# Sequence-mixing block and window attention on one core: start of the scan by half sequences, B of four units in float32, split of B, decay ring and mlp additions in another order

## What is computed

```
block 0 (per image, L = 1024 positions, E = 192 inner channels, N = 16 states)
  xn  = layernorm over channels(x) * gamma + beta          # forward and reversed: 8 sequences
  xr  = silu(causal conv of 4 taps(xn @ W_in[:, :E]) + conv_b);   z = xn @ W_in[:, E:]
  dbl = xr @ W_xproj                                       # rank 6 | B (16) | C (16)
  dt  = softplus(dbl[:6] @ W_dt + b_dt)
  h_t = exp(dt_t * A[n]) * h_(t-1) + dt_t * xr_t * B_t[n]    # for each channel and state n
  y_t = sum over n of C_t[n] * h_t[n] + D * xr_t
  x   = x + 0.5 * (forward + reversed)((y * silu(z)) @ W_out)
block 1 (4 images, 6 heads of 16 channels)
  qkv = conv1x1(batchnorm(x)); scores = 7x7 conv of (q, k) -> 49 weights per head and position
  out = softmax(scores) . the 7x7 window of v; x = x + proj(out); x = x + c2(gelu(c1(x)))
```

## Time and profile before

| | before |
|---|---|
| median of 3 runs | 1159.88 us |
| the profiled execution, its own time | 1160.85 us |
| its span | 1159.1 us |
| first scan of unit 0 starts | 59.52 us |
| last scan (unit 191) starts | 745.79 us |
| attention's first instruction | 756.17 us |
| mean granted TensorE clock | 0.944 |
| PE, DVE, ACT, POOL busy | 1048.3, 919.1, 571.7, 918.2 us |

### The profile page before, as it was taken

How to read it: one execution, slowest core, us unless ns; L and a number is a source line. 1 busy time by engine, 2 the same in 40 slices (tenths; PEclk the granted TensorE clock), 3 DMA queues, 4 the chain that set the end, 5 groups by cost and what they waited for, 6 DMA issues and landing times. The chain is left out here.

```text
span 1159.1 us, 9592 instructions
## 1 busy us (share of the span) xinstructions
PE 1048.3 (90%) x3268; PEld 371.8 (32%) x3268; DVE 919.1 (79%) x598; ACT 571.7 (49%) x601; POOL 918.2 (79%) x369
## 2 busy tenths in 40 slices
PE   7889999899999999998987888979999999997865
PEld 2223333233333323333333323323333333332321
DVE  1299998869998989998898999920197978979881
ACT  5766859598866666766667654322112020110411
POOL 0079999989998979999899998610098999899890
PEclk8879999989999989999999999969999999999778
DMA  3234556633555554755354655368475678936002
GB/s 86 95 125 148 191 158 168 196 135 128 201 171 160 163 168 130 187 165 201 127 198 140 190 160 195 113 145 174 86 138 126 120 143 152 159 69 107 23 0 77
DMA packets 112769, 162.78 MB, mean 140 GB/s; under 512 B 63962, under 2 KB 76992, under 8 KB 112720
## 3 DMA queue, kind: packets, MB, share of 16 engines
q1 hardware_dynamic: 109264, 155.17, 50.2%
q10 hardware_dynamic: 3456, 6.99, 2.1%
HBM read 137.43 MB, written 11.23 MB: 128 GB/s over the span
## 5 line engine op out<-in xcount | busy, mean ns | idle before, releaser
L750 POOL TENSOR_TENSOR hc<-h,c_rep 128x1024 f32<-128x1024 f32 x191 | 447.2, 2359 | 104.4 <-DVE h L803 93.1
L803 DVE TENSOR_TENSOR_SCAN h<-a,bu 128x1024 f32<-128x1024 f32 x192 | 436.8, 2284 | 31.9 <-ACT bu L631 9.8
L452 PE MATMUL y_ps<-hc,ident 128*128 128x512 f32 x768 | 380.7, 620 | 0.8 <-DVE hc L851 0.3
L621 ACT ACTIVATE a<-dt,a_neg 128x1024 f32<-128x1024 f32 x192 | 216.6, 1143 | 133.7 <-DVE h L803 130.9
L790 DVE TENSOR_TENSOR bu<-bu,u 128x1024 f32<-128x1024 f32 x165 | 199.6, 1210 | 20.9 <-PE bu L422 20.8
L452 PEld LDWEIGHTS y_ps<-hc,ident 128*128 128x128 f32 x768 | 144.8, 195 | 203.0 <-issue 183.2
L1248 POOL TENSOR_TENSOR prod_p<-vw,at 128x3584 f32<-128x3584 f32 x18 | 130.4, 7243 | 93.5 <-ACT at L1209 92.2
L1128 PE MATMUL sc_ps<-x,w_up 128*64 128x480 f32 (+3 forms) x672 | 142.9, 576 | 0.0
L1128 PE MATMUL sc_ps<-x,w_low 96*64 96x480 f32 (+6 forms) x672 | 136.5, 556 | 0.0
L422 PE MATMUL bu<-st,pick 96*128 96x512 bf16 (+1 forms) x438 | 101.5, 389 | 35.9 <-DVE h L803 34.2
L1198 ACT ACTIVATE sc<-sc_ps,rel 128x512 f32<-128x512 f32 x24 | 16.5, 687 | 237.8 <-PE sc_ps L1128 237.8
(11 more groups left out here) (129 smaller groups left out, 993.4 us busy)
## 6 DMA issues: line engine op xcount, KB each, us to landing
c_rep<-bc_d SPq DMA_DIRECT2D x128, 512.0 KB, 3.8
c_rep<-bc_d SPq DMA_DIRECT2D x128, 256.0 KB, 4.0
vw<-v_d SPq DMA_DIRECT2D x24, 532.0 KB, 9.3
x<-qk SPq DMA_DIRECT2D x66, 140.0 KB, 3.9
b_rep<-bc_d SPq DMA_DIRECT2D x17, 512.0 KB, 4.8
b_rep<-bc_d SPq DMA_DIRECT2D x20, 256.0 KB, 5.1
scores_d<-sc ACTq DMA_DIRECT2D x48, 98.0 KB
at<-scores_d SPq DMA_DIRECT2D x48, 98.0 KB, 3.9
```

The costliest lines, as they stand in the source:

```text
L452: mm = pe.matmul(y_ps[:, cols(th)], ident[:, :], hc[:, k % HC_RING, cols(th)], start=(n == 0 and d == 0), stop=(n == N_ST - 1))
L621: nc.scalar.activation(a[:, k % A_RING, :], dt[:, tile % 2, :], ACT.Exp, scale=a_neg[:, kind_of(tile), n:n + 1]).then_inc(exp_done, 1)
L750: nc.gpsimd.tensor_tensor(hc[:, k % HC_RING, :], h[:, k % H_RING, :], c_rep[:, k % C_RING, :], ALU.mult).then_inc(hc_done, 1)
L803: nc.vector.tensor_tensor_scan(scan_order(h[:, k % H_RING, :], d), scan_order(a[:, k % A_RING, :], d), scan_order(bu[:, k % 2, :], d), 0.0 ...
```

## The change

1. The loads: the first group keeps x of image 0 and `center`; gamma and beta go to the second.
2. The start by half sequences (512 positions): squares and scalings on DVE, Ln, Exp and the affine on ACT by halves; a second buffer `var_1` (it lies in `hc`) for image 1; `w_taps` is made by POOL instead of DVE; conv of tile 0's first half is issued before the variance of image 1; tile 2's silu is taken straight out of PSUM by halves; softplus of tile 0 by halves on ACT and DVE, with its u.
3. Units 0 to 3 spread B from `dbc` in float32 with `pick_f` (two matmuls), so they need no split; the split of sequence 0 is made by ACT and POOL behind the first two decays, in buffers of its own (`st_left` lies in `hc`). conv of tile 1 still stands before the first spread in PE's queue.
4. `A_RING` 3 to 4: the decay is issued three units ahead instead of two.
5. `PLAN`: xp and dt of sequence 1 / tile 1 one unit later. `middle` 5 units after its job instead of 2, `lowest` 6 instead of 2 (for the job's end at unit e: `rest` e+1, `middle` e+5, `lowest` e+6); `affine` 4 instead of 3; B of the POOL units loaded and multiplied four units ahead instead of three.
6. Attention: `mlp_out` sits behind a row's product; image 0's first pair goes from after tile 4 to row (4, 3), its second pair from after the tile to row (5, 0), image 1's first pair from row (5, 0) to (5, 1); image 2's last pair from before to after the division of tile 5. The sum of the weights and its reciprocal come after row 0.

```diff
-A_RING, H_RING, HC_RING, C_RING, SUM_LAG = 3, 4, 4, 4, 3
+A_RING, H_RING, HC_RING, C_RING, SUM_LAG = 4, 4, 4, 4, 3
-LOADS = [4, 7, 12, 8]
+LOADS = [2, 9, 12, 8]
-DVE_MLP = {(4, WIN): ((0, 0),), (4, WIN + 1): ((0, 8),), (5, 0): ((1, 0),), (5, 2): ((1, 8),), (5, 3): ((2, 0),),
-           (5, WIN): ((2, 8),)}
+DVE_MLP = {(4, 3): ((0, 0),), (5, 0): ((0, 8),), (5, 1): ((1, 0),), (5, 2): ((1, 8),), (5, 3): ((2, 0),)}
-    (0, "xp", 1, 0, 0), (2, "xp", 1, 0, 1), (5, "dt", 1, 0), (6, "dt", 1, 1), (7, "conv", 3, 0), (11, "conv", 3, 1),
+    (1, "xp", 1, 0, 0), (3, "xp", 1, 0, 1), (6, "dt", 1, 0), (7, "dt", 1, 1), (7, "conv", 3, 0), (11, "conv", 3, 1),
-B_RING, B_AHEAD, B_LOAD = 2, 3, 3
+B_RING, B_AHEAD, B_LOAD = 2, 4, 4
+MID_LAG, LOWEST_LAG = 5, 6
...
+                if k < EARLY:
+                    for th in range(2):
+                        mm = pe.matmul(bu[:, k % 2, cols(th)], pick_f[0:2 * N_ST, n:n + 1].to_broadcast([2 * N_ST, 128]),
+                                       dbc[0:2 * N_ST, 0, cols(th)], start=True, stop=True)
+                    mm.then_inc(spread, 1)
+                    return
...
+            for th in range(2):
+                norm_job("cen", 0, th)
+            for th in range(2):
+                norm_job("var", 0, th)
+            pe.wait_ge(loaded[1], 16 * LOADS[1])
+            for th in range(2):
+                norm_job("cen", 1, th)
+            pe.wait_ge(taps_ready, 2)
+            for j in range(TAPS):
+                conv_job(0, 0, j)
+            for th in range(2):
+                norm_job("var", 1, th)
+            for tile, th in ((0, 1), (2, 0), (2, 1)):
+                for j in range(TAPS):
+                    conv_job(tile, th, j)
...
+            def soft_half_logs(th):
+                half = cols(th)
+                act.wait_ge(job_done, J("dt", 0, th))
+                nc.scalar.activation(t3[:, half], bank("dt", 0, th), ACT.Abs, bias=b_dt[:, 0:1]).then_inc(abs_half, 1)
+                act.wait_ge(abs_half, th + 1)
+                nc.scalar.activation(t3[:, half], t3[:, half], ACT.Exp, scale=-1.0).then_inc(soft_act, 1)
+                nc.scalar.activation(dt[:, 0, half], bank("dt", 0, th), ACT.Relu, bias=b_dt[:, 0:1])\
+                    .then_inc(left_act, 1)
+                act.wait_ge(soft_act, 2 * th + 1)
+                nc.scalar.activation(t4[:, half], t3[:, half], ACT.Ln, bias=1.0).then_inc(soft_act, 1)
...
             for th in range(2):
                 center_left(0, th)
             for th in range(2):
-                variance_left(0, th)
+                variance_half(0, th)
+            act.wait_ge(loaded[1], 16 * LOADS[1])
             for th in range(2):
                 center_left(1, th)
-            affine(0)
-            for th in range(2):
-                variance_left(1, th)
-            affine(1)
+                affine_half(0, th)
...
+            conv_left(0, 0)
+            for th in range(2):
+                variance_half(1, th)
+            for th in range(2):
+                affine_half(1, th)
+            conv_left(0, 1)
+            silu(0)
+            for th in range(2):
+                leave(("conv", 2, th), xr_of(2)[:, cols(th)], bank("conv", 2, th), ACT.Silu, bias=conv_b[:, 1:2])
+            nc.scalar.preload_act_table_set("natural_log_exp_and_others")
+            for th in range(2):
+                xp_left(0, 0, th)
+            for th in range(2):
+                soft_half_logs(th)
+            nc.scalar.activation(st[:, 0, :], dbc[0:ROWS - RANK, 0, :], ACT.Copy).then_inc(st_high, 1)
             act.wait_ge(set_up, 3)
+            for k in range(2):
+                decay(k)
             middle(0, 0)
             for th in range(2):
                 conv_left(1, th)
+            for k in range(2, A_RING - 1):
+                decay(k)
             silu(1)
             nc.scalar.preload_act_table_set("natural_log_exp_and_others")
             for k in range(UNITS):
                 copy_y(k)
                 copy_b(k + 1)
-                decay(k + 2)
+                decay(k + A_RING - 1)
                 front(k)
...
-                    if done + 2 == k and name == "xp" and job[2] == 1:
+                    if done + MID_LAG == k and name == "xp" and job[2] == 1:
                         middle(*job[0:2])
...
-                        if done + 2 == k:
+                        if done + LOWEST_LAG == k:
                             lowest(nc.gpsimd, pool, SEQS.index(tuple(job[0:2])))
...
+            pool.wait_ge(loaded[1], 16 * LOADS[1])
+            for part in range(2):
+                j = slice(2 * part, 2 * part + 2)
+                nc.gpsimd.tensor_tensor(w_taps[:, j, :], conv_w_rows[:, j, :],
+                                        w_in.unsqueeze(1).broadcast_to([C, 2, E_IN]), ALU.mult)\
+                    .then_inc(taps_ready, 1)
+            rest(nc.gpsimd, pool, 0)
+            lowest(nc.gpsimd, pool, 0)
+            pool.wait_ge(st_done, 1)
...
                 for dy in range(DVE_ROWS[j]):
-                    for m, i in DVE_MLP.get((j, dy), ()):
-                        mlp_out(m, i)
-                        mlp_out(m, i + 1)
                     row(j, dy)
-                for m, i in DVE_MLP.get((j, WIN), ()):
-                    mlp_out(m, i)
-                    mlp_out(m, i + 1)
+                    if dy == 0:
+                        nc.vector.tensor_reduce(den[:, 0, :], at[:, j % 2].rearrange("p k x -> p x k"), AX.X, ALU.add)\
+                            .then_inc(soft, 1)
+                        dve.wait_ge(soft, 3 * j + 2)
+                        nc.vector.reciprocal(den[:, 1, :], den[:, 0, :]).then_inc(soft, 1)
...
-            for i in (0, 1, 8, 9):
-                mlp_out(B - 1, i)
+            for m, i in ((2, 8), (2, 9), (3, 0), (3, 1), (3, 8), (3, 9)):
+                mlp_out(m, i)
```

More of the change, by code:

```diff
@@ L229, in left, with x_ready @@
             eng.wait_ge(left_dve if JOBS[n - 1][0] == "out" else left_act, len(same))
+        def x_ready(eng, t):
+            if t == 2:
+                left(eng, J("conv", 2, 1))
+            else:
+                eng.wait_ge(xr_ready, max(CONVS.index(t), 1))
         def xr_of(t):
@@ L243, in _ @@
             groups = [
-                [(x1[:, 0, :], t["x"][0]), (center[:, :, :], t["center"]), (norm[:, 0:1], t["gamma"]),
-                 (norm[:, 1:2], t["beta"])],
-                [(x1[:, 1, :], t["x"][1]),
+                [(x1[:, 0, :], t["x"][0]), (center[:, :, :], t["center"])],
+                [(x1[:, 1, :], t["x"][1]), (norm[:, 0:1], t["gamma"]), (norm[:, 1:2], t["beta"]),
                  (conv_w_rows.rearrange("p j e -> p (j e)"), t["conv_w"].to_broadcast([C, TAPS * E_IN])),
@@ L317, in norm_job @@
                     pe.wait_ge(squared, 2 * b + th + 1)
-                    pe.matmul(bank(name, b, th)[0:C, :], center[:, 1, :], var[:, cols(th)], start=True,
+                    squares = var_1 if b == 1 else var
+                    pe.matmul(bank(name, b, th)[0:C, :], center[:, 1, :], squares[:, cols(th)], start=True,
                               stop=True).then_inc(job_done, 1)
@@ L327, in conv_job @@
                     free(J("conv", tile, th))
-                    pe.wait_ge(normalised, (i if kind == "L" else 2 * i + 1) + 1)
+                    b = i if kind == "L" else 2 * i + 1
+                    if b >= 2:
+                        pe.wait_ge(normalised, b - 1)
+                    elif tile < 3:
+                        pe.wait_ge(normal_half, 2 * b + th + 1)
+                    else:
+                        pe.wait_ge(normal_half, 2 * b + 2)
                 if kind == "L":
@@ L413, in spread_b @@
                 tile, n = divmod(k, N_ST)
-                if n == 0:
+                if n == 0 and tile or k == EARLY:
                     for s in tile_seqs(tile):
@@ L515, in variance_left, with variance_half, affine_half @@
                     nc.scalar.activation(var[:, :], var[:, :], ACT.Exp, scale=-0.5).then_inc(inverse, 1)
+            def variance_half(b, th):
+                half = (var_1 if b == 1 else var)[:, cols(th)]
+                leave(("var", b, th), half, bank("var", b, th)[0:C, :], ACT.Ln, bias=norm[:, 2:3])
+                left(act, J("var", b, th))
+                nc.scalar.activation(half, half, ACT.Exp, scale=-0.5).then_inc(inverse_half, 1)
+            def affine_half(b, th):
+                act.wait_ge(scaled_half, 2 * b + th + 1)
+                nc.scalar.activation(xi(b, cols(th)), xi(b, cols(th)), ACT.Identity, scale=norm[:, 0:1],
+                                     bias=norm[:, 1:2]).then_inc(normal_half, 1)
+            def soft_half_logs(th):
[8 more added lines that the diff above has]
+                nc.scalar.activation(t4[:, half], t3[:, half], ACT.Ln, bias=1.0).then_inc(soft_act, 1)
             def affine(b):
-                act.wait_ge(scaled, b + 1)
+                act.wait_ge(scaled, b - 1)
```

(23 more changed lines are left out.)

116 lines of the change are left out of this document (69 added, 47 removed).

## The result

The changed kernel takes **1142.73 us**, the median of 4 runs (1141.05 to 1144.43); the kernel before, run beside it on the same chip, 1159.96. The ratio is 0.985, with an interval of 0.983 to 0.9869. On the profiled executions it went from 1160.85 to 1141.05 us, and the span from 1159.1 to 1139.2.

The account below looks back on a forecast made before the run. Bound by a start chain alternating engines, nearly full DVE and POOL with stalls in the scan stage, then PE and POOL in attention. 10.5 - 0.5 + 11 - 2.2 + 2.1 + 0.7 = 21.6 less: 1138.3 us median, range 1128 to 1150.

Parts of the forecast that it names:

- (a): Start: PE's first matmul waits for `center` instead of beta, so 4.3 us instead of 5.29.
- (b): Start: norm by halves, four half tiles of conv at 3.55 us each; ends at 30.2 against 35.33.
- (e): Start: conv of tile 1 from 36.7, 10.25 or 7.1 us long; first scan 9.5 to 12.7 earlier, 10.5 taken.
- Rival (2): All fits: full clock in conv of tile 1 and the projection, scan stage gains 17; 1128.9 us, chance 0.15.
- (d): Start: softplus of tile 0 by halves; u complete at 42.6 us instead of 54.12.
- (f): Units 0 to 3: float32 spreads take 1.75 us at full clock, 3.5 at half; cost 0 to 3, 0.5 taken.
- Rival (4): Start gives its gain back: half-clock spreads and PE's backlog hold units 1 to 8; about 1153.3 us, chance 0.10.
- (h): Tile 1: softplus one unit later with `lowest` among it; a stall of 3.3 us, net 2.2 slower.
- (g): Scan stage: ACT no longer waits for POOL's `rest`, DVE's stalls shrink; 0 to 23 us gained, 11 taken.
- rival 1: Scan stage: POOL takes over and gives DVE's stalls back; gain 2 instead of 11, 1147.3 us, chance 0.22.
- (i) and (j): Attention, tile 5: POOL ends 3.1 us earlier, DVE waits 4.7 for image 1's last pair; 2.1 gained.
- (k): End of attention: image 3's projection comes packed behind image 2's mlp; 0 to 1.4 us more, 0.7 taken.

Follow-up runs that it names:

- lags: Kernel before with only the middle part of the split five units after its xp job and the lowest six, instead of two; 1147.52 us, ratio 0.9914.
- old plan: Changed kernel with xp and dt of sequence 1 / tile 1 at the units of before (0, 2, 5, 6); 1138.98 us, ratio 0.9836.
- `EARLY` = 2: Changed kernel with float32 spreads of B for units 0 and 1 only, instead of 0 to 3; 1138.24 us, ratio 0.9819.
- Put together: Changed kernel, unit 0's spread ahead of tile 1's conv, POOL's subtraction behind u, two float32 spreads, tile 1's xp and dt units of before; 1132.4 us.

## Why the prediction was right, and where it was off

The direction, the size and the condition on the distance from the first scan to the last (668 to 686; it is 676.64) held. Its other condition did not: it called itself wrong if the first scan came later than 52, and that came at 54.11. Step by step:

**(a) to (e), the start: 10.5 taken, 5.4 measured.** (a) held, 4.55 against 4.3. The term that was mis-sized is the first half tile of conv in (b): 3.55 taken from PE at full clock, 5.71 measured, since the clock had not yet risen. Where it rose at 13.9 the same half tile takes 3.67, and the first scan of the same start is at 52.09 (old plan): 2 us of the miss are this, and still less than the forecast is gained. The other way round, the 59.52 of before is of an execution in which the clock fell again; against the 56.1 of the kernels with lags or attention alone, whose start is the same, the 5.4 is 2.0. conv of tile 1 began at 40.58 instead of 36.7, and (e)'s slow end of 10.25 held (10.18). Rival (2) had this conv at full clock and 12.7 instead of 10.5. It was not: the wait ahead of it was 1.16 us for the 1.3 foreseen, the granted clock was 1.00 in 28 to 36 us and 0.50 in 40 to 44, and this conv took 10.10 to 10.59 us in all eight other executions with the new start. That fewer waits ahead of it would bring the full clock no run shows. u was complete at 48.59 instead of the 42.6 of (d), partly by the 1.75 us that DVE's subtraction lost beside POOL. PE's conv and spread hid that in the changed kernel.

**(f) 0.5 taken, 3.6 measured.** From unit 0 to unit 9 the scans take 34.58 us instead of 31.02. Its own upper bound was 3. The term's price is the float32 spread at the lower clock, 3.77 us each beside the xp pieces at 2.03; with two of them instead of four the same stretch takes 30.6. Rival (4) had this mechanism right.

**(h) 2.2 taken, 2.9 measured** between units 9 and 16, and the stall of 3.3 before unit 16 came as 3.23. Its cause is the one named: the softplus that starts a unit later (old plan: no stall), of which moving `lowest` alone took away 1.2.

**(g) 11 taken, 16.1 measured.** From unit 16 to the last scan it is 614.2 instead of 630.4, and 614.4 in the kernel without the start. "Half" between 0 and 23 was too careful. The lags alone bring 10.2 there and the ring alone 3.9; the other 2 are left to `affine`, `B_AHEAD` and what the edits do to each other, which was not tried apart. POOL did not take over (rival 1): its busy time in the stage stays at 642 us while the stage gets shorter, so POOL's idle time inside it falls from 46.9 us (688.6 - 641.7) to 37.1 (678.9 - 641.85), and to 32.7 without the new start. The row of the table by stretch for the changed kernel's stage:

```profile
54.10:733.00 678.90, 633.14 (x1659) 229.64 (x1658) 632.84 (x367) 463.15 (x468) 641.85 (x279) 0.97 0.55 167
```
POOL's 641.85 is the last of the five busy times. The forecast that POOL would wait less than 20 us for DVE was wrong (28.3): DVE's stalls had cost POOL only part of its slack.

**(i) and (j) held.** POOL's tile 5 begins right behind tile 4, DVE waits 4.63 for 4.7 foreseen, and from the end of PE's scores to the last division it is 67.0 us instead of 69.2, so 2.2 less for 2.1. **(k)** 0.7 taken, 1.9 measured from the last division to the end. How much it brings differs from execution to execution: where PE stood 0.45 us ahead of image 3's projection that took 1.93 us, where it stood 2.61, in the kernel with `EARLY` = 2, 3.70 (granted clock 0.50 from 1119.5 to 1126.2), and its whole end is 4.2 us longer. The wait alone does not settle it: behind 1.85 us it took 3.28 with attention alone, behind 1.97 in the kernel of "Put together" 1.93.

**The balance.** The scan of unit 16 starts at 116.53 in the changed kernel and at 115.44 in the one before: the start, the largest part of the diff, had lost all its lead and 1.1 us more before the second tile began; against 112.06 in the kernel with attention alone, where the start of before fared better, it is 4.5 more. For the start the forecast had 10.5 - 0.5 - 2.2, so 7.8 us gained. Without it the rest of the change runs at a ratio of 0.9794 instead of 0.985, so it cost some 6.5 us: the sign was wrong. The 17 us come from the other edits, the lags and the ring above all, and attention, which bring about 24 by themselves and had been put at 13.8. That the two errors nearly cancel is luck. Whether the start is of use at all depends on what stands in PE's queue in its first units; with the spread ahead of conv, two float32 spreads and the old plan, unit 16 starts at 106.2, 10.3 us ahead of the changed kernel, and 9.3 of that reach the last scan. Even so its time can't be told from that of the kernel without the start, so no run shows a clear gain from the start.

## What to carry to other kernels

A stage that starts earlier is a gain only as far as the queue it starts into lets it run: price the first units after the edit at the clock and with the queue that they will have, not only the chain up to the first one. Follow the lead through checkpoints (here units 0, 9, 16, 96, the last); where it is lost is where the next edit belongs. A wait of an engine with idle time for another one (ACT for POOL here) is often removed by moving the waiting instruction three units back, and here those two lines were worth more than the whole rewritten start.

## What the runs showed of the hardware

- **DVE and POOL.** A DVE subtraction of two SBUF tiles, 128x512, took 2.44 or 2.45 us beside a POOL subtraction of 2.12 in all six executions in which they met, ending 0.55 us behind it in the changed kernel, and 0.69 in the three in which POOL's was moved. DVE's products of a PSUM tile with u keep their 1.21 to 1.23 us beside POOL's products. Why the one is held up and the others are not, these runs do not show.
- **The clock's first rise moves, and the start with it.** The clock records of the changed kernel's trace begin at 19.4 us. Ahead of its first record the table by stretch prints 1.00 although nothing is recorded there. The matmuls show the level: records of 96x512 in float32 take 1.06 us up to 18.0 and 0.59 from 19.6 on, and in the kernel before they take 1.06 us where a clock of 0.50 is on record:

```profile
16.37 3.70 PE L318 MATMUL f_ps<-var,center 96*96 96x512 f32 x4 [2.06 <-ACT var L509]
```

```profile
16.00:20.00 4.00, 3.63 (x5) 1.34 (x6) 0.00 (x0) 3.05 (x5) 0.00 (x0) 0.50 0.64 165
```

So the half tile of conv at 15.31, 5.71 us, ran for the most part at the lower level, and the one at 22.74, 3.62 us, at the full one. The kernel with the spread ahead of conv has the same instructions up to there, and its first clock record begins at 14.0:

```profile
15.31 3.67 PE L353 MATMUL f_ps<-xn,w_taps 96*128 96x512 f32 x8 [0.50 <-ACT xn L564]
```

- **The start of before comes out in two ways too.** Where the clock rose at 12.4 or 12.5 us and fell to 0.50 from 15.9 to 22.7, conv of tile 1 took 10.25 or 10.41 us (first scan 59.5 and 59.4); where it rose at 14.4 to 15.3 and stayed at 1.00 past 41, 8.83 (56.1, 56.1 and 55.7). The profile of before that the prediction rests on is of the first kind, so 3.4 us of the room at the start are not always there. What decides when the clock rises is not shown by these runs.
